# Another order of the attention units in a fused cross-attention and top-2 expert kernel, and another order of its prologue

## The chip, the cores and the metric

The kernel runs on one core of a Trainium2 chip. The metric is the device time of one execution in microseconds. Five engines work side by side, each on its own queue of instructions: TensorE (PE) for matrix products, VectorE (DVE), ScalarE (ACT), GpSimd (POOL), and SyncE (SP), which here only issues DMAs. They are kept in order by semaphores.

## What is computed

128 sequences of 64 tokens with 128 channels, float32. A causal cross-attention with 16 heads of 64, then a layer norm and a top-2 mixture of 8 experts.

```python
x = x + xattn(_layernorm(x), ctx, ctx)      # qh = q @ Wq, kh = k @ Wk, vh = v @ Wv; softmax(qh kh^T / 8, causal) vh @ Wo + bo
z = _layernorm(x'); z2 = _layernorm(z) * ln_g + ln_b   # x' = x after attention; the expert layer norms again
w = top2(softmax(z2 @ rW + rb)), normalised to 1
x = x' + z + sum_e w_e * (gelu(z2 @ W1[e] + b1[e]) @ W2[e] + b2[e])
```

## The kernel before

Two sequences make a pair of 128 tokens; there are 64 pairs, in 16 groups of four (`GP`, `NG`). Products of queries, keys and values are made of float32r parts ("high" and "low", three matmuls for one product, `split_product`, L903 to L909).

The attention work of a pair is cut into **units**, each of which fills one of five PSUM banks used in turn (`RING`). A unit's bank comes free when the unit five places earlier in `ORDER` has been evicted. The units of pair i of a group are: P (transposes of z and context, in pairs 0 and 2 only), V0 and V1 (values of the pair), K0 to K3 (in pairs 0 and 2 the queries, in pairs 1 and 3 the keys of the next two pairs), T0 and T1 (transposes of the softmax of the pair before), O0 and O1 (output of `attend` for the pair before), and the routing units RZ, RX, RL of the group before. `pair_units` (L49 to L52) writes the order; TensorE, ScalarE and VectorE each walk through it with their own code in `group`. ScalarE evicts the V, K, T and O units, makes the exponentials (`exp_half`) and seeds the score banks with the mask (`seed`). VectorE makes the maxima, differences and the normalising of the softmax. Groups 0, 1 and 15 are written out, groups 2 to 14 run in a loop on each engine.

TensorE's order for a pair n is: P, V0, `scores(n)`, `project(n-2)`, K0, T0, K1, T1, (RZ or RX), K2, K3, V1, `attend(n-1)`, (RL). `scores` (L1034) and `attend` (L1005) are 32 matmuls of 64x64 each, float32, which the profile shows as 64 records; `project` (L1018) is the product with Wo.

GpSimd normalises the inputs of the next group (`prep`), makes the rows for the experts, and sends them to DRAM with eight indirect scatters for each group, one after each unit named in `send_at` (L619). In the loop: one when the slots are known, then on O31, P0, V00, T00, O00, V10 and T11.

The prologue loads x, Wq, Wk, the context and Wv, splits the weights (ScalarE high parts L731 and L736, VectorE low parts), transposes P2 (L933, L936), transposes the small vectors b1, ln_g, ln_b (L1107), and computes eight key units before group 0. After the attention, 71 tiles of 256 rows go through the experts; that stage is not touched.

## Time and profile before

| | |
|---|---|
| three timed runs | median 1069.29 us (1067.63 to 1070.48) |
| the profiled execution | 1062.37 us, span 1060.6 us |
| busy, share of span: TensorE, VectorE, ScalarE, GpSimd | 85%, 69%, 58%, 46% |
| mean granted TensorE clock | 0.931 |

The profile is one execution. A row of the timeline says when a group of equal instructions started, how long it lasted from first start to last end, its engine, its line of the kernel, what it wrote and read, how many there were, and in brackets how long the engine stood before and what released it. "Issue" means that the profile shows nothing it waited for. A matmul's end is modelled and overlaps the next start. PEld is TensorE's weight load. SPq is the time in which the queue of SP issues a DMA.

### The profile page before, as it was taken

Reading aid. Unit: us, or ns where it says so; the run is one execution under the profiler, and the core shown is the slowest. Engines: PE = TensorE matmul, PEld = TensorE weight load, DVE = VectorE, ACT = ScalarE, POOL = GpSimd, SP = SyncE. Lnnn points to the kernel's source line nnn. Section 1 sums busy time; section 2 is a strip of 40 time slices with the busy share of each in tenths; the row PEclk is TensorE's granted clock in tenths of the full one; section 3 lists DMA queues with packets and bytes.
Section 4 is the critical chain, followed back from the end, with each engine's and each line's share of the span. In section 5 each row is a group of like instructions: output and inputs, shape, how many; then the busy total and the mean of one; then the engine's idle time right before and its main releaser. Section 6 shows DMA issues by size and latency. Waiting matters only on the chain.

```text
span 1060.6 us, 36484 instructions
## 1 busy us (share of the span) xinstructions
PE 900.8 (85%) x13361; PEld 787.1 (74%) x13361; DVE 735.7 (69%) x2239; ACT 615.3 (58%) x1317; POOL 484.4 (46%) x580
## 2 busy tenths in 40 slices
PE   5999899999999999999999999999677577777770
PEld 4889788888878888888888888888566466666660
DVE  3977787777777877777777787868376544445663
ACT  3677666666665765765675675765254243344463
POOL 3612536434363543536444363523345655555551
PEclk8999999999999999999999999999689788788885
DMA  9000101101010010101001010000123322224665
GB/s 276 23 22 2 38 16 32 32 8 35 5 37 30 13 32 8 35 8 37 30 10 35 5 35 22 13 13 10 41 61 94 89 74 73 77 78 137 171 185 193
DMA packets 55664, 56.63 MB, mean 53 GB/s; under 512 B 7335, under 2 KB 48593, under 8 KB 55601
## 3 DMA queue, kind: packets, MB, share of 16 engines
q1 hardware_dynamic: 46651, 37.94, 12.6%
q0 software_dynamic: 8640, 17.84, 5.0%
q8 instruction: 30, 0.49, 0.2%
q14 instruction: 33, 0.27, 0.1%
q10 hardware_dynamic: 310, 0.08, 0.0%
HBM read 32.62 MB, written 23.23 MB: 53 GB/s over the span
## 4 chain that ended last, share of the span: by engine, by line
PE 65%; DVE 12%; issue 10%; ACT 5%; another core or an unknown queue 5%; DMA 2%; DVEq 0%; SPq 0%; ACTq 0%; POOL 0%; POOLq 0%
PE bank L905 10%; PE bank L1018 9%; PE bank L909 9%; PE bank L906 8%; PE bank L1034 7%; PE bank L1005 7%; PE bank L1159 5%; PE bank L988 4%; DVE mx L1272 2%; PE bank L1136 2%; DVE pr L1274 2%; ACT pr L850 1%; PE bank L958 1%; PE bank L933 1%
## 5 line engine op out<-in xcount | busy, mean ns | idle before, releaser
L905 PE MATMUL bank<-in_h,Ah 128*128 128x256 f32 x654 | 213.3, 326 | 39.6 <-DVE Al L1562 12.7
L773 ACT ACTIVATE pr<-pr 128x512 f32<-128x512 f32 x128 | 80.9, 632 | 240.9 <-DVE pr L1274 240.9
L701 POOL DMA_INDIRECT mixed<-kf,ix_i x142 | 139.6, 983 | 110.5 <-DVE ix_i L1579 68.4
L905 PEld LDWEIGHTS bank<-in_h,Ah 128*128 128x128 f32 x654 | 130.2, 199 | 49.9 <-issue 21.6
L725 ACT ACTIVATE kf<-bank 128x512 f32<-128x512 f32 x256 | 155.1, 607 | 11.5 <-PE bank L909 11.1
L909 PE MATMUL bank<-in_h,Al 128*128 128x256 f32 x512 | 145.8, 285 | 0.0
L906 PE MATMUL bank<-in_l,Ah 128*128 128x256 f32 x512 | 145.4, 284 | 0.0
L615 POOL DMA_INDIRECT slots<-zrow,slot_ix x120 | 126.2, 1052 | 40.1 <-issue 28.9
L1272 DVE TENSOR_REDUCE mx<-bank 128x8 f32<-128x512 f32 x128 | 87.8, 686 | 77.1 <-PE bank L1034 76.9
L1018 PE MATMUL bank<-wo_s,oT 128*128 128x128 f32 x1024 | 135.7, 287 | 2.7 <-ACT oT L768 2.3
L550 POOL TENSOR_TENSOR idle_p<-half 128x1 f32<-128x1 f32 x114 | 26.1, 229 | 231.9 <-DVE slot_ix L1365 186.1
L1034 PEld LDWEIGHTS bank<-kf 64*64 64x64 f32 x4096 | 81.7, 137 | 66.2 <-issue 65.0
L1018 PEld LDWEIGHTS bank<-wo_s,oT 128*128 128x128 f32 x1024 | 123.2, 197 | 7.3 <-ACT oT L768 2.7
L1034 PE MATMUL bank<-kf 64*64 64x64 f32 x4096 | 101.6, 226 | 30.9 <-issue 29.5
L1284 DVE TENSOR_TENSOR pr<-pr,ri 128x512 f32<-128x512 f32 x128 | 121.3, 947 | 4.4
L1159 PE MATMUL bank<-kf,pr 128*128 128x128 f32 x568 | 96.6, 322 | 31.2 <-ACT pr L850 29.5
L1159 PEld LDWEIGHTS bank<-kf,pr 128*128 128x128 f32 x568 | 81.9, 222 | 42.2 <-ACT pr L850 31.6
L555 POOL TENSOR_TENSOR rs<-ve,half 128x4 f32<-128x4 f32 (+1 forms) x32 | 43.5, 1360 | 139.0 <-DVE ve L1213 99.7
L850 ACT ACTIVATE pr<-bank,kf 128x256 f32<-128x256 f32 x142 | 59.8, 476 | 68.9 <-remote 40.5
L906 PEld LDWEIGHTS bank<-in_l,Ah 128*128 128x128 f32 x512 | 98.8, 193 | 0.0
L909 PEld LDWEIGHTS bank<-in_h,Al 128*128 128x128 f32 x512 | 98.1, 192 | 0.0
L1274 DVE TENSOR_TENSOR pr<-bank,mx 128x512 f32<-128x512 f32 x128 | 88.5, 692 | 4.4
(191 smaller groups left out, 1949.6 us busy)
## 6 DMA issues: line engine op xcount, KB each, us to landing
kf<-slots SPq DMA_DIRECT2D x71, 130.0 KB
kf<-mixed SPq DMA_DIRECT2D x12, 512.0 KB, 3.7
xs<-in_x_dram SPq DMA_DIRECT2D x16, 256.0 KB
c_in<-in_ctx_dram SPq DMA_DIRECT2D x16, 256.0 KB
out_dram<-xs SPq DMA_DIRECT2D x16, 256.0 KB
mixed<-kf,ix_i POOLq DMA_INDIRECT x142
vf<-mixed SPq DMA_DIRECT2D x4, 512.0 KB
slots<-zrow,slot_ix POOLq DMA_INDIRECT x120
```

Of the source, the lines that this page charges most:

```text
L615: pool.indirect_dma_start(out=slots, out_offset=bass.IndirectOffsetOnAxis(ap=ix[:, k, t:t + 1], axis=0), in_=rows[:, t, :], in_offset=None ...
L701: pool.indirect_dma_start(out=mixed, out_offset=bass.IndirectOffsetOnAxis(ap=ix_i[buf][:, j:j + 1], axis=0), in_=y_sb[buf][:, j, :], in_of ...
L725: act.activation(kfs[par][:, 2 * u:2 * u + 2, :], ring[gr.bank(name)].rearrange("p (h t) -> p h t", h=2), ACT.Copy).then_inc(act_ev, 1)
L905: pe.matmul(ps, lh, rh, start=True, stop=False)
L906: pe.matmul(ps, lh, rl, start=False, stop=False)
L909: return pe.matmul(ps, ll, rh, start=False, stop=True)
L1018: last = pe.matmul(o_ps[:, 0:D], oT[:, j, :], wo_s[:, j, :], start=(j == 0), stop=(j == H // 2 - 1))
L1034: last = pe.matmul(s_ps[b][place, S * j:S * j + S], kfs[par][dims, j, toks], kfs[par][dims, H // 2 + j, toks], start=False, stop=True, ski ...
L1159: last = pe.matmul(into[:, j, :], hid[deep][:, c, j * P:(j + 1) * P], w_f[deep][:, c * D:(c + 1) * D], start=False, stop=(c == FC - 1), sk ...
L1272: dve.reduce_max(mx[:, par, hs], src, AX_X).then_inc(sm_st, 1)
L1274: dve.tensor_tensor(by_seq(par, t), src, mx[:, par, hs].unsqueeze(2).to_broadcast([P, 8, S]), ALU.subtract).then_inc(shifted, 1)
L1284: dve.tensor_tensor(by_seq(par, t), by_seq(par, t), ri[:, par, hs].unsqueeze(2).to_broadcast([P, 8, S]), ALU.mult).then_inc(probs, 1)
```

## The change

In the attention the two transposed halves of the softmax (T) come directly behind the scores of the next pair, `project` after them, and `attend` comes between K1 and K2. ScalarE's order follows, and five of the scatters are tied to other units. In the prologue the transpose of the small vectors moves behind the first scores; seven warming matmuls take its place; the product for rb joins `fold_b1`; the statistics of group 1 move to the end of the first pair on VectorE; the second x load and the load of b2 are issued earlier; ScalarE splits Wv after it has evicted P2; and GpSimd's split of W1 is cut by expert. The lines that begin with # inside the diff name the place.

```diff
 def pair_units(i):
-    return p + [v[0], k[0], t[0], k[1], t[1]] + routing + [k[2], k[3], v[1]] + o + (["RL"] if i == 2 else [])
+    return p + [v[0]] + t + [k[0], k[1]] + routing + o + [k[2], k[3]] + (["RL"] if i == 2 else []) + [v[1]]
...
+        vec_at, rb_at, b1_at = (bank[7][:, at:at + n] for at, n in ((0, E * FC + 2), (32, E), (64, E * FC)))
...
# SP, prologue (behind the two mask loads)
+            sp.wait_ge(st_ok, 9)
+            sp.dma_start(xs[:, GP:2 * GP, :], x_t[:, GP:2 * GP, :]).then_inc(ld_x, 16)
+            sp.dma_start(experts[0:3, :, 2 * HF + B2:], b2.rearrange("(a e) d -> a e d", a=1).to_broadcast([3, E, D])).then_inc(ld_v, 16)
             sp.dma_start(rb_b[:, :], rb.rearrange("(a d) -> a d", a=1).to_broadcast([P, E])).then_inc(ld_v, 16)
             sp.dma_start(rW_s[:, :], rW).then_inc(ld_v, 16)
             sp.dma_start(w1_raw[:, :, :], W1.rearrange("e d f -> d e f")).then_inc(ld_b, 16)
             sp.dma_start(wo_s[:, :, :], Wo.rearrange("(j p) n -> p j n", p=P)).then_inc(ld_w[3], 16)
-            sp.dma_start(experts[0:3, :, 2 * HF + B2:], b2.rearrange("(a e) d -> a e d", a=1).to_broadcast([3, E, D])).then_inc(ld_v, 16)
...
-            sp.wait_ge(st_ok, 9)
-            sp.dma_start(xs[:, GP:2 * GP, :], x_t[:, GP:2 * GP, :]).then_inc(ld_x, 16)
...
# GpSimd, split_w1: three instructions become 24
-                high, low = experts[:, :, 0:HF], experts[:, :, HF:2 * HF]
-                pool.tensor_scalar(low, high, gc, None, ALU.mult).then_inc(e1_ok, 1)
...
+                high, low = ([experts[:, e, at:at + HF] for e in range(E)] for at in (0, HF))
+                for e in range(E):
+                    pool.tensor_scalar(low[e], high[e], gc, None, ALU.mult).then_inc(e1_ok, 1)
+                for e in range(E):
+                    pool.wait_ge(e1_ok, e + 1)
+                    pool.tensor_copy(high[e].bitcast(F32R), low[e]).then_inc(e1_ok, 1)
+                for e in range(E):
+                    pool.wait_ge(e1_ok, E + e + 1)
+                    pool.tensor_tensor(low[e].bitcast(F32R), low[e], high[e], ALU.subtract).then_inc(e1_ok, 1)
...
# GpSimd, group loop (the same renaming before and behind the loop)
-                send_at(g - 2, group_of(g - 1), "O31", 1)
+                send_at(g - 2, group_of(g - 1), "V31", 1)
                 send_at(g - 2, gr, "P0", 2)
                 prep(g + 1, gr.done("P0"), between=lambda: send_at(g - 2, gr, "V00", 3),
-                     ahead=lambda: send_at(g - 2, gr, "T00", 4))
-                send_at(g - 2, gr, "O00", 5)
+                     ahead=lambda: send_at(g - 2, gr, "K00", 4))
+                send_at(g - 2, gr, "V01", 5)
                 x1_centre(g - 1)
                 send_at(g - 2, gr, "V10", 6)
-                send_at(g - 2, gr, "T11", 7)
+                send_at(g - 2, gr, "K11", 7)
...
# ScalarE, one pair; split_v moves behind input_unit(start, "P2", 0)
-                    exp_half(n, par, 0)
                     value_unit(gr, f"V{i}0", n, par)
+                    if attends:
+                        for t in range(2):
+                            t_unit(gr, f"T{i}{t}", n - 1, t)
+                    exp_half(n, par, 0)
                     exp_half(n, par, 1)
...
                         seed(n + 1, 0)
                     if keyed:
-                        key_unit(gr, f"K{i}2")
+                        key_unit(gr, f"K{i}1")
+                    if i == 2 and not first:
+                        r_unit(gr)
                     if seeds:
                         seed(n + 1, 1)
+                    if attends:
+                        for b in range(2):
+                            heads_unit(gr, f"O{i}{b}")
                     if keyed:
+                        key_unit(gr, f"K{i}2")
                         key_unit(gr, f"K{i}3")
                     value_unit(gr, f"V{i}1", n, par)
...
# TensorE, one pair
                     scores(n, i)
+                    if first and i == 0:
+                        vector_columns()
...
+                    if attends:
+                        for t in range(2):
+                            t_half(gr, f"T{i}{t}", n - 1, 1 - par, t)
                     if not (first and i < 2):
                         project(n - 2, gr.done(f"O{i - 1}1", 0) if i else kept.done("O31", 0))
...
                         key_unit(gr, f"K{i}0")
...
+                        key_unit(gr, f"K{i}1", (lambda: heads_free(gr, i)) if attends else None)
+                    elif attends:
+                        heads_free(gr, i)
                     if i == 2 and not first:
                         r_transposes(gr, r)
                     if i == 3 and not first:
                         r_ranks(gr, r)
+                    if attends:
+                        attend(gr, i, 1 - par)
                     if keyed:
                         key_unit(gr, f"K{i}2")
                         key_unit(gr, f"K{i}3")
...
                     if i == 2 and not first:
                         r_logits(gr)
+                    value_unit(gr, f"V{i}1", i)
+                    if not attends:
+                        fold_b1()
...
# TensorE, prologue
             input_unit(start, "P2", 0, 0)
-            pe.wait_ge(ld_v, 16 * 6)
+            warm(7)
             pe.wait_ge(pro_l, 4)
-            pe.transpose(bank[7][:, 0:E * FC + 2], vec_rows[:, :],
-                         ident[0:E * FC + 2, 0:E * FC + 2]).then_inc(vec_ps, 1)
...
# VectorE, first pair of the first group, behind its two shift halves
+                    if first and i == 0:
+                        dve.wait_ge(vec_ps, 1)
+                        dve.tensor_copy(vec_cols[:, :], vec_at).then_inc(vec_ok, 1)
+                        dve.wait_ge(vec_ok, 1)
+                        dve.tensor_copy(bc_wide[:, :], bc.to_broadcast([P, P])).then_inc(vec_ok, 1)
...
# VectorE, end of that pair
                     if first and i == 0:
-                        dve.wait_ge(fold_ps, 2)
+                        prep_stats(1)
+                        dve.wait_ge(fold_ps, 1)
+                        dve.tensor_tensor(rb_sum[:, :], rb_at, rb_b[:, :], ALU.add).then_inc(fold_ok, 1)
+                        dve.tensor_scalar(rW_g[:, :], rW_s[:, :], gc, None, ALU.mult).then_inc(w1_ok, 1)
```

## Rows read from the trace of the kernel before

**Rows 1.** Busy windows: start:end, length, busy us per engine, granted clock, DMA share, GB/s.

```profile
18.00:20.00 2.00, 1.36 (x6) 1.32 (x7) 0.93 (x5) 0.00 (x0) 0.00 (x0) 0.50 1.10 344
...
300.00:400.00 100.00, 93.27 (x1684) 82.61 (x1683) 76.19 (x209) 66.58 (x132) 46.16 (x58) 1.00 0.08 23
```

**Rows 2.** Timeline of TensorE, loop pair 0: start, us, line, tiles, count [idle before].

```profile
338.73 0.43 PE L933 MATMUL bank<-ident,z 128*128 128x128 f32 x2 [0.20 <-ACT kf L725]
...
340.01 0.92 PE L1034 MATMUL bank<-kf 64*64 64x64 f32 x40
...
342.76 2.05 PE L1018 MATMUL bank<-wo_s,oT 128*128 128x128 f32 x16
...
345.72 0.36 PE L905 MATMUL bank<-in_h,Ah 128*128 128x256 f32 x1
345.92 0.28 PE L906 MATMUL bank<-in_l,Ah 128*128 128x256 f32 x1
346.04 0.29 PE L909 MATMUL bank<-in_h,Al 128*128 128x256 f32 x1
...
349.18 1.16 PE L1005 MATMUL bank<-pT,vf 64*64 64x64 f32 x64
```

**Rows 3.** Timeline of TensorE, loop pairs 1 and 3.

```profile
305.60 0.92 PE L1034 MATMUL bank<-kf 64*64 64x64 f32 x46
...
307.34 2.05 PE L1018 MATMUL bank<-wo_s,oT 128*128 128x128 f32 x16
...
328.81 1.16 PE L1034 MATMUL bank<-kf 64*64 64x64 f32 x64
...
335.05 0.38 PE L905 MATMUL bank<-in_h,Ah 128*128 128x256 f32 x1 [0.61 <-ACT kf L725]
```

**Rows 4.** Timeline of GpSimd beside them: the indirect scatters.

```profile
305.61 0.98 POOL L615 DMA_INDIRECT slots<-zrow,slot_ix  x1 [0.48 <-issue]
...
339.42 0.98 POOL L615 DMA_INDIRECT slots<-zrow,slot_ix  x1 [0.48 <-PE bank L936]
...
340.80 0.99 POOL L615 DMA_INDIRECT slots<-zrow,slot_ix  x1 [0.16 <-issue]
...
346.80 1.43 POOL L615 DMA_INDIRECT slots<-zrow,slot_ix  x1 [0.32 <-issue]
```

**Rows 5.** Timeline of all engines, first scatter of the kernel.

```profile
105.79 1.67 POOL L615 DMA_INDIRECT slots<-zrow,slot_ix  x1 [0.65 <-issue]
...
106.40 1.39 PE L1005 MATMUL bank<-pT,vf 64*64 64x64 f32 x64
```

**Rows 6.** Timeline of all engines, prologue.

```profile
9.40 0.38 PE L936 MATMUL bank<-ident,c_in 128*128 128x128 f32 x2
...
9.71 3.78 SPq L399 DMA_DIRECT2D experts<-in_L_ffn_b_dram  x1
...
10.95 0.58 ACT L718 ACTIVATE in_h<-bank 128x512 fp32r<-128x512 f32 x1
...
11.56 0.69 DVE L1260 TENSOR_TENSOR in_l<-bank,in_h 128x512 fp32r<-128x512 f32 x1 [1.40 <-ACT in_h L718]
...
18.64 0.29 PE L1107 MATMUL bank<-ident,vec_rows 18*128 18x18 f32 x1 [8.86 <-DMA experts<-in_L_ffn_b_dram]
...
26.40 0.29 PE L1118 MATMUL bank<-rW_s,bc_wide 128*128 128x8 f32 x2
...
28.24 1.16 PE L1034 MATMUL bank<-kf 64*64 64x64 f32 x64
```

**Rows 7.** Timeline of VectorE, last step of the softmax of loop pair 1.

```profile
314.47 0.98 DVE L1284 TENSOR_TENSOR pr<-pr,ri 128x512 f32<-128x512 f32 x1
```

**Rows 8.** Timeline of all engines, last group.

```profile
747.74 0.79 PE L909 MATMUL bank<-Vh,in_l 128*128 128x512 f32 x1 [3.29 <-ACT pT L754]
...
749.68 0.69 DVE L1284 TENSOR_TENSOR pr<-pr,ri 128x512 f32<-128x512 f32 x1
...
755.21 1.06 PE L988 MATMUL bank<-ident,pr 128*128 128x128 f32 x4
```

More of the change, by code:

```diff
@@ L652, in _ @@
             send(0, upto=1)
-            send_at(0, group_of(1), "O31", 1)
+            send_at(0, group_of(1), "V31", 1)
             send_at(0, group_of(2), "P0", 2)
             prep(3, group_of(2).done("P0"), between=lambda: send_at(0, group_of(2), "V00", 3),
-                 ahead=lambda: send_at(0, group_of(2), "T00", 4))
-            send_at(0, group_of(2), "O00", 5)
+                 ahead=lambda: send_at(0, group_of(2), "K00", 4))
+            send_at(0, group_of(2), "V01", 5)
             x1_centre(1)
             send_at(0, group_of(2), "V10", 6)
-            send_at(0, group_of(2), "T11", 7)
+            send_at(0, group_of(2), "K11", 7)
             z2_rows(1)
@@ L677, in _ @@
             send(NG - 3, upto=1)
-            send_at(NG - 3, group_of(NG - 2), "O31", 1)
-            for q, name in enumerate(("P0", "V00", "T00", "O00")):
+            send_at(NG - 3, group_of(NG - 2), "V31", 1)
+            for q, name in enumerate(("P0", "V00", "K00", "V01")):
                 send_at(NG - 3, end, name, q + 2)
@@ L819, in _ @@
             input_unit(start, "P2", 0)
+            split_v()
             for k in range(4):
@@ L1051, in key_unit, with vector_columns @@
                     last = split_product(ring[gr.bank(name)][:, SUB * a:SUB * (a + 1)], Ah[:, 2 * u + a, :],
-                                         Al[:, 2 * u + a, :], in_h[par][:, src, :], in_l[par][:, src, :])
+                                         Al[:, 2 * u + a, :], in_h[par][:, src, :], in_l[par][:, src, :],
+                                         ahead if a else None)
                 last.then_inc(unit, 1)
+            def vector_columns():
+                pe.wait_ge(ld_v, 16 * 6)
+                pe.transpose(vec_at, vec_rows[:, :], ident[0:E * FC + 2, 0:E * FC + 2]).then_inc(vec_ps, 1)
             def fold_b1():
+                pe.wait_ge(vec_ok, 2)
+                pe.matmul(rb_at, bc_wide[:, :], rW_s[:, :], start=True, stop=True)
                 pe.wait_ge(ld_b, 16)
                 for u in range(E * FC):
-                    last = pe.matmul(bank[7][:, u:u + 1], w1_raw[:, u // FC, (u % FC) * P:(u % FC + 1) * P], bc,
+                    last = pe.matmul(b1_at[:, u:u + 1], w1_raw[:, u // FC, (u % FC) * P:(u % FC + 1) * P], bc,
                                      start=True, stop=True)
@@ L1074, in group @@
                     scores(n, i)
+                    if first and i == 0:
+                        vector_columns()
                     keyed = not (last and i >= 2)
+                    attends = not (first and i == 0)
+                    if attends:
+                        for t in range(2):
+                            t_half(gr, f"T{i}{t}", n - 1, 1 - par, t)
                     if not (first and i < 2):
@@ L1114, in _ @@
                 key_unit(start, f"K3{k}")
-            pe.wait_ge(vec_ok, 2)
-            pe.wait_ge(ld_w[3], 16)
-            pe.matmul(bank[7][:, 0:E], bc_wide[:, :], rW_s[:, :], start=True, stop=True).then_inc(fold_ps, 1)
             group(0, first=True)
@@ L1459, in group @@
                     n, par = GP * g + i, i % 2
-                    if i == 0 and not last:
+                    if i == 0 and not first and not last:
                         prep_stats(g + 1)
-                        if not first:
-                            mask_tables(g + 1)
+                        mask_tables(g + 1)
                     if i == 2 and not first and not second:
```

53 lines of the change are left out of this document (10 added, 43 removed).

## The prediction

> **What bounds the kernel now.** I read the busy windows first. In a stretch of the attention loop TensorE is busy 93 of 100 us at the full granted clock, VectorE 76, ScalarE 67 and GpSimd 46 [rows 1]. So only two things can change the time of the loop: what TensorE must do, and the seven per cent in which it stands still. The same view shows the second place to look: at 18 to 20 us the granted clock is 0.50 and TensorE has hardly worked.
>
> Then I read TensorE's rows for one pair [rows 2]. The 64 records of `scores` start at 340.01 and `project` follows at 342.76: 2.75 us. Undisturbed, the same 64 records take about 1.1 us (the 328.81 row lasts 1.16 with the tail of its last matmul) [rows 3]. In the next pair they take 1.74 us [rows 3]. The lost time, 1.65 and 0.65 us, has no releaser; it is "issue". I compared these places with GpSimd's rows [rows 4]. One scatter runs at 305.61, with the 1.74 us scores. Two run at 339.42 and 340.80, around the 2.75 us scores, and none is near 328.81. My reading: **while GpSimd makes an indirect scatter, TensorE gets its instructions slowly.** A store of some 35 to 45 small matmuls is used up and the rest waits until about 0.3 us after the scatter. Long matmuls hide this, a burst of 64 short ones does not. `scores` and `attend` are such bursts. The only `attend` that a scatter meets (105.79) took 1.39 instead of 1.16 us [rows 5].
>
> In the third pair the scores meet two scatters as in the first (its rows are left out; I count the same 1.65), in the fourth none. So a turn of the loop loses 0.65 + 2 x 1.65 = 4.0 us this way. In the fourth pair there is a real wait, too: K32 stands 0.61 us for ScalarE's eviction of K30 [rows 3].
>
> In the prologue the chain is short [rows 6]. TensorE has transposed P2 at 9.8 and then stands 8.86 us for the transpose of `vec_rows`, which waits for the small load of b2 (issued at 9.71, taking 3.78 us of SP). All eight key units stand behind it, and the first ones run at half clock. Scores of pair 0 start at 28.24.
>
> **The change, part by part.**
>
> *Prologue.* `vector_columns` goes behind the first scores. The first key unit then needs in_h, in_l and the weights' low parts. In_h was late, behind Vh on ScalarE (10.95); now it comes first: 9.8 + 0.58 for in_h, + 0.69 for in_l gives 11.1 [rows 6]. The seven warm matmuls add little (estimate 1.5 us from 9.8, so 11.3) and keep the clock up. Eight key units and that transpose took 26.40 - 18.64 = 7.8 us, the first half of them at clock 0.50. At the full clock a unit is six steps of 0.12 [rows 2], so eight are 5.9. P0 and V00 with the wait for kf and seeds took 1.84 (26.40 to 28.24). New start of the scores: 11.3 + 5.9 + 1.8 = 19.0, that is **-9.2**. Beside it the seeds need the mask tables, now about 14.5 (VectorE does Vl first), if the masks have landed; no row shows when. SP's order: the x load and b2 go ahead of rb, rW, W1, Wo and the expert weights, which are issued up to 4 us later (3.78 + 0.5). W1 is wanted by `fold_b1` only behind scores, four key units and V01, at about 24. Bound: between -6 (something lands late) and -10. The transposed column and the rb product only move: +0.3 in all. `prep_stats(1)` moves behind the first softmax, so GpSimd's prep(1) and its split of W1 end later against TensorE; P2 wants z about 10 us after. The split in 24 pieces lets VectorE in between; VectorE is not the bound. I take **-9.0**.
>
> *Type changes on TensorE.* The first key matmul after a transpose steps 0.20 instead of 0.12 us [rows 2]. Both transposes now follow the scores and precede `project`, so two such changes go per pair. One change comes back where `attend` is followed by K2. V1 is followed by V0 or P instead of `attend`. Over the four pairs I count -0.3 us a turn, between 0 and -0.6.
>
> *The wait in the fourth pair.* K32 takes the bank of K30, and now `attend` lies between them: 1.1 us of cover. The wait of **0.61** goes. Next late would be route_a, whose logits come 0.8 earlier because RL now stands before V21.
>
> *Scores against scatters.* The sends are renamed so that they fire at about the same moments (V31 ends the group as O31 did). Scatter 1 comes 0.7 us after the pair's start and the second one 1.4 later [rows 2, 4]. The loss in pairs 0 and 2 therefore stays. In pair 1 V10 no longer follows `attend`, so the scores start 0.1 earlier against the scatter: -0.1.
>
> *Attend against scatters.* This is new. The fifth scatter stands at 346.80, 8.07 us after the pair's start, and takes 1.43 [rows 4]. Today key units lie there, and `attend` comes at 349.18 [rows 2]. In the new order `attend` starts at 1.28 (P0, V00) + 2.75 (scores) + 2.96 (project, K00 and T00, from 342.76 to 345.72) + 0.35 (T01, as T00) + 0.8 (K01, as K00) = 8.15 [rows 2]. They meet almost exactly. The price has no row in this position. Below it is bounded by 0 (nothing is gained, since an undisturbed `attend` has no stall to lose; the store lasts: `attend` is 1.1 long and the store covers the first 0.6 to 0.8), above by 1.0 (the scatter lasts to 9.5, +0.3, +the rest). The nearest rows give 0.23 [rows 5] and 0.65 [rows 3]. I take **+0.5**.
>
> A turn: -0.61 - 0.3 - 0.1 + 0.5 = -0.5; thirteen turns are **-6.6**, between +0.3 and -13. Groups 0 and 1 run outside the loop and before the scatters: -1.2 (one wait, seven pairs of type changes).
>
> *A wait that moves.* T(n-1) is now asked right after the scores of n, and project(n-2) is queued behind it. It waits for VectorE's softmax of n-1. VectorE ends the softmax of pair 1 at 315.45, 8.1 us after its scores' end at 307.34, the longest of a turn [rows 3, 7]. A pair without lost time is about 9.5 us from scores' end to scores' end (342.76 to 349.18, then 1.1 for attend, 0.9 for V0, 1.1 for scores) [rows 2]. So at least 1.4 us of cover is left; pair 2's scores lose 1.65 more. I cost it at nothing. VectorE's addition of `project` comes 2.7 us after the scores' end and `project` now ends 2.6 after it: level.
>
> *The end.* In the last group no keys fill TensorE. V31 waits 3.29 us for pT [rows 8], because ScalarE takes the exponentials of the last pair before the transposes. The new order takes the transposes first. Next late is then RX, which waits for the routing, and after that the transposes of pair 63: its softmax ends at 750.4, while they start at 755.21 today behind project(62) [rows 8]. So no more than 4.8 us can go here. The scatters of group 14 still meet the last `attend`. I take **-3.5**, between 0 and -4.8.
>
> The expert stage is untouched and moves as a whole. **Sum:** -9.0 - 1.2 - 6.6 - 3.5 = -20.3. The profiled execution took 1062.4 us (span 1060.6), which gives 1042.1. It lies 6.9 us below the median of the timed runs, 1069.3; against that the forecast is 1069.3 - 20.3 = **1049**.
>
> A page speaks of the same "issue" time. The Trainium skill, "Runtime: NRT & Kernel Launch", section "Instruction fetch mechanics", says that each engine fetches its code in 16 KiB blocks and that an issue floor of about 20 cycles an instruction hides the fetching. By that rule bursts would run at the pace of the issuing side, and two bursts close together (`attend`, then `scores`) would run it dry, scatter or none. The undisturbed row [rows 3] has an `attend` just before it, too, and doesn't agree. The rival that follows from the rule is the first below.
>
> **The rivals.**
> 1. *The store is not full when the scores begin,* because `attend` emptied it 1 to 2 us before. Then putting K2, K3 and V1 between the bursts as well, 15 long matmuls, heals both. For: each disturbed burst of scores follows an `attend`. Against: the attend of rows 5 follows no burst and still lost time. It would give back 4.0 and the 0.5 a turn: 13 x 4.5 = 59, so 990. Chance 0.08.
> 2. *Attend pays in full* (1.0 a turn: +6.5) and the end gives nothing (+3.5): 1059. Chance 0.15.
> 3. *The prologue's gain is not there,* since masks, seeds or W1 arrive no earlier (they come behind the attention weights in the queue), and rival 2 as well: 1067 to 1069. Chance 0.08.
> 4. *Slower: the transposes in front.* If VectorE's softmax is more than 1.4 us later than today against TensorE (GpSimd's tensor work holding it up, a later `project` holding the addition), T and with it project, keys and all wait in each pair. It decides from 1.4 us on; each further us costs about 60 us over the 63 pairs. With 0.5 us over it: 1049 + 30 = 1079. For: project and K0, 2.6 us, no longer cover the wait. Against: TensorE is busy 93% and VectorE 76% [rows 1]. Chance 0.09.
>
> My forecast has 0.60, with a range of its own of 1042 to 1056.
>
> **How the numbers follow.** The low end takes attend at 0 (-6.5), the end at -4.8 and the prologue at -10: 1040. The high end holds rival 2 and a prologue of -6: 1061. Left out are rival 1, rival 4 and most of rival 3. About 0.3% (3 us) is what a measurement of this kernel can tell from no change. Faster: forecast, rivals 1 and 2 and a little of 3: 0.84. Same 0.07, slower 0.09.
>
> **What would show it.** Prologue: first key matmul near 11.3, first scores near 19, granted clock 1.00 between 10 and 20 us. Loop: a turn shorter by 0.5 us; no wait at K32; scores of pairs 0, 1 and 2 as long as today; the attend of pair 0 about 1.6 long with an "issue" gap. End: no 3.29 us wait for pT. I am wrong if the scores lose no time any more (rival 1), if T waits for VectorE (rival 4), or if scatters have moved onto other bursts.

## The result and the profile after

The changed kernel is slower. Its median is 1078.25 us of 9 runs (1073.58 to 1081.31); the kernel before, run beside it, has 1069.29 (1065.42 to 1070.92). The ratio is 1.011, with a 95% interval of 1.0086 to 1.0134. I had forecast 1049 and faster. Where the executions of a kernel fall into two sets, as those of project_first and fifth_scatter_later do below, medians and ratios are of the faster set (eight of twelve, 1057.8 to 1070.6 us, and five of twelve, 1049.4 to 1061.9; the others reach 1088.5 and 1076.7, one stands at 2735.6).

The profiled execution of the changed kernel took 1076.2 us, its span is 1074.4. That is 13.8 us over the span of the kernel before (1060.6). Four moments split these 13.8 us: the first scores, the first scores of the loop, the last scores, and the first matmul of the expert stage. Timeline of TensorE, changed kernel (start, length, engine, line, operation, count):

```profile
18.85 1.16 PE L1038 MATMUL bank<-kf 64*64 64x64 f32 x64
...
99.10 0.90 PE L1038 MATMUL bank<-kf 64*64 64x64 f32 x37
...
751.05 1.16 PE L1038 MATMUL bank<-kf 64*64 64x64 f32 x64
...
780.22 1.06 PE L1143 MATMUL bank<-ident,kf 128*128 128x128 f32 x4
```

The same moments of the kernel before (the first is the 28.24 of [rows 6]):

```profile
113.19 1.56 PE L1034 MATMUL bank<-kf 64*64 64x64 f32 x48
...
738.78 1.16 PE L1034 MATMUL bank<-kf 64*64 64x64 f32 x64
...
768.28 1.06 PE L1136 MATMUL bank<-ident,kf 128*128 128x128 f32 x4
```

| stretch | before | after | difference | forecast |
|---|---|---|---|---|
| to the first scores | 28.24 | 18.85 | -9.4 | -9.0 |
| groups 0 and 1 | 84.95 | 80.25 | -4.7 | -1.2 |
| loop and last group | 625.59 | 651.95 | +26.4 | -6.6 |
| last scores to expert stage | 29.50 | 29.17 | -0.3 | -3.5 |
| expert stage | 292.3 | 294.2 | +1.9 | 0 |

So the prologue did what it should, and everything is lost in the loop. A turn of the loop (four pairs) took 45.6 us and takes 47.8 now; these are medians of the 13 turns of each profiled execution.

Pair 0 shows most of it. TensorE of the changed kernel, scores of pair 0 to the attend behind them; this stretch answers to [rows 2]:

```profile
523.72 0.81 PE L1038 MATMUL bank<-kf 64*64 64x64 f32 x40
524.84 0.31 PE L1038 MATMUL bank<-kf 64*64 64x64 f32 x2 [0.31 <-issue]
525.59 0.30 PE L1038 MATMUL bank<-kf 64*64 64x64 f32 x2 [0.44 <-issue]
526.34 0.61 PE L1038 MATMUL bank<-kf 64*64 64x64 f32 x20 [0.45 <-issue]
526.88 1.97 PE L990 MATMUL bank<-ident,pr 128*128 128x128 f32 x8
528.64 2.74 PE L1022 MATMUL bank<-wo_s,oT 128*128 128x128 f32 x16
531.14 0.36 PE L907 MATMUL bank<-in_h,Ah 128*128 128x256 f32 x1
...
532.73 1.22 PE L1007 MATMUL bank<-pT,vf 64*64 64x64 f32 x54
534.30 0.42 PE L1007 MATMUL bank<-pT,vf 64*64 64x64 f32 x10 [0.35 <-issue]
```

Beside it GpSimd, the indirect scatters:

```profile
523.49 0.99 POOL L615 DMA_INDIRECT slots<-zrow,slot_ix  x1 [0.48 <-PE bank L938]
...
524.87 0.99 POOL L615 DMA_INDIRECT slots<-zrow,slot_ix  x1 [0.16 <-issue]
...
532.93 1.35 POOL L615 DMA_INDIRECT slots<-zrow,slot_ix  x1 [0.48 <-issue]
```

Two things are to be seen. The scores take 3.16 us to the next operation, 2.75 before: the first scatter starts 0.23 us ahead of them and not 0.59, so the second one, too, ends later against the burst, and the burst ends about 1.0 us after the second scatter in both kernels (525.86 to 526.88; 341.79 to 342.76). Pairs 1 and 2 show the same: their scatters start 0.20 and 0.34 us later against the scores than before, and the bursts are 0.17 and 0.38 us longer. And behind the burst the transposes and the projection last 1.97 and 2.74 us. In the next group of rows the reason stands: the granted clock is 0.50 there (526.90). Busy windows of the changed kernel (start:end, length, busy us per engine, granted clock, DMA share, GB/s):

```profile
200.00:700.00 500.00, 464.87 (x7891) 419.27 (x7893) 367.52 (x1034) 332.18 (x628) 217.74 (x273) 0.97 0.07 21
...
146.40:149.80 3.40, 3.40 (x40) 3.33 (x32) 2.92 (x6) 2.05 (x4) 3.20 (x5) 1.00 0.32 103
...
526.90:530.30 3.40, 3.40 (x18) 3.40 (x17) 3.09 (x5) 1.92 (x4) 3.20 (x5) 0.50 0.28 77
```

and of the kernel before, the loop and the stretch behind the same scores (340.01):

```profile
200.00:700.00 500.00, 466.13 (x8308) 413.50 (x8307) 387.54 (x1089) 331.71 (x659) 227.48 (x285) 1.00 0.07 23
...
342.70:346.10 3.40, 3.40 (x37) 3.34 (x30) 3.18 (x6) 1.60 (x3) 3.20 (x5) 1.00 0.27 87
```

The changed kernel falls to the lower of the two clock levels (1.2 for 2.4 GHz) in the last eleven of the 13 turns of the loop and once more in the last group, each time behind pair 0's scores; in the kernel before no fall starts in the loop. From the first transpose to the first key matmul it is 4.26 us (526.88 to 531.14); in pair 1 of the group before, at the full clock, the same steps take 2.63 (491.85 to 494.48). A fall costs 1.6 us. The second turn of the changed kernel says the same: its scores of pair 0 (143.35) are held up as long, 3.01 us, the clock stays at 1.00 behind them (146.40 above), and the turn takes 46.1 us; the next one has a fall and takes 47.7.

A turn with a fall then adds up, pair by pair (scores to scores, before and after): 11.2 and 13.95, 10.6 and 10.7, 12.6 and 13.0, 11.2 and 10.1. By cause: +1.6 for the clock; +0.95 for longer scores in pairs 0, 1 and 2 (first to last start 3.04, 1.80, 3.16 us for 2.64, 1.63, 2.78; 0.94 undisturbed); +0.83 for the attend of pair 0 (1.77 for 0.94), which the scatter at 532.93 meets; -1.1 in pair 3, where the waits at K32 and P0 are gone. That is +2.3 of the measured +2.2.

### The profile page after: what moved, and what is told of

Same layout as the page of the kernel before. It is cut to its first block, busy times and chain, and to the rows that moved or that the text cites. A ratio compares the mean times of both kernels' runs of the same rounds, so it can differ in the third digit from the quotient of the medians.

```text
span 1074.4 us, 36492 instructions
## 1 busy us (share of the span) xinstructions
PE 914.0 (85%) x13368; PEld 811.1 (75%) x13368; DVE 729.0 (68%) x2239; ACT 636.8 (59%) x1317; POOL 488.1 (45%) x601
## 4 chain that ended last, share of the span: by engine, by line
PE 75%; issue 8%; another core or an unknown queue 6%; DVE 5%; ACT 3%; DMA 1%; POOL 1%; DVEq 0%; POOLq 0%; ACTq 0%; SPq 0%
PE bank L1022 11%; PE bank L907 11%; PE bank L911 9%; PE bank L908 9%; PE bank L1038 9%; PE bank L990 7%; PE bank L1007 7%; PE bank L1166 5%; PE bank L1143 2%; ACT pr L852 1%; PE bank L960 1%; PE bank L1161 1%; PE bank L935 1%; PE bank L938 1%
## 5 line engine op out<-in xcount | busy, mean ns | idle before, releaser
L907 PE MATMUL bank<-in_h,Ah 128*128 128x256 f32 x654 | 207.7, 318 | 24.5 <-DVE Al L1569 10.8
L728 ACT ACTIVATE kf<-bank 128x512 f32<-128x512 f32 x256 | 148.0, 605 | 26.0 <-PE bank L911 20.5
L756 ACT ACTIVATE pT<-bank 128x512 f32<-128x512 f32 x128 | 70.9, 595 | 152.3 <-PE bank L990 152.3
L615 POOL DMA_INDIRECT slots<-zrow,slot_ix x120 | 126.0, 1050 | 42.3 <-issue 30.8
L1038 PEld LDWEIGHTS bank<-kf 64*64 64x64 f32 x4096 | 84.2, 135 | 76.0 <-issue 75.8
L1038 PE MATMUL bank<-kf 64*64 64x64 f32 x4096 | 105.7, 226 | 40.7 <-issue 40.7
L1022 PEld LDWEIGHTS bank<-wo_s,oT 128*128 128x128 f32 x1024 | 131.9, 208 | 10.5 <-ACT oT L770 10.5
L1291 DVE TENSOR_TENSOR pr<-pr,ri 128x512 f32<-128x512 f32 x128 | 110.4, 863 | 4.4
```

Of the source, the lines that this page charges most:

```text
L615: pool.indirect_dma_start(out=slots, out_offset=bass.IndirectOffsetOnAxis(ap=ix[:, k, t:t + 1], axis=0), in_=rows[:, t, :], in_offset=None ...
L728: act.activation(kfs[par][:, 2 * u:2 * u + 2, :], ring[gr.bank(name)].rearrange("p (h t) -> p h t", h=2), ACT.Copy).then_inc(act_ev, 1)
L907: pe.matmul(ps, lh, rh, start=True, stop=False)
L1022: last = pe.matmul(o_ps[:, 0:D], oT[:, j, :], wo_s[:, j, :], start=(j == 0), stop=(j == H // 2 - 1))
L1038: last = pe.matmul(s_ps[b][place, S * j:S * j + S], kfs[par][dims, j, toks], kfs[par][dims, H // 2 + j, toks], start=False, stop=True, ski ...
L1291: dve.tensor_tensor(by_seq(par, t), by_seq(par, t), ri[:, par, hs].unsqueeze(2).to_broadcast([P, 8, S]), ALU.mult).then_inc(probs, 1)
```

## The experiments

All ratios are to the kernel before, run on the same chip. A turn is read between the scores of pair 0 in consecutive groups of the profiled execution; the table has the median of the 13 turns of the loop, and in how many of them the clock fell. The kernel before has 45.6 and 0, the changed kernel 47.8 and 11.

| kernel | median us | ratio, 95% interval | turn | turns with a fall |
|---|---|---|---|---|
| prologue_alone | 1057.7 | 0.992 (0.9892 to 0.9949) | 45.7 | 1 |
| changed_again | 1077.0 | 1.0097 (1.0066 to 1.0129) | 47.7 | 13 |
| project_first | 1063.2 | 0.9974 (0.9944 to 1.0004) | 46.1 | 2 |
| fifth_scatter_later | 1057.6 | 0.9919 (0.9883 to 0.9956) | 47.7 | 11 |
| both_small | 1041.6 | 0.9749 (0.9725 to 0.9774) | 44.4 | 0 |
| two_moved | 1020.9 | 0.962 (0.9594 to 0.9645) | 44.4 | 8 |
| tail_held | 1059.6 | 0.9992 (0.9967 to 1.0018) | 47.6 | 11 |
| after_retimed | 1009.6 | 0.9492 (0.9459 to 0.9526) | 42.3 | 0 |
| after_clean | 1015.8 | 0.9581 (0.9555 to 0.9607) | 43.6 | 1 |
| after_spaced | 1001.9 | 0.9376 (0.9352 to 0.9401) | 42.1 | 1 |
| first_order_clean | 1040.6 | 0.9816 (0.9793 to 0.9839) | 44.9 | 3 |
| first_order_spaced | 1053.8 | 0.9874 (0.9853 to 0.9895) | 45.8 | 1 |
| exps_first | 1091.7 | 1.0242 (1.0216 to 1.0267) | 48.5 | 11 |
| first_order_exps_later | 1036.2 | 0.9712 (0.9687 to 0.9737) | 44.5 | 0 |

**The parts and the clock.**

```diff
 project_first: in every pair
-t_half(T0), t_half(T1); project(n - 2)
+project(n - 2); t_half(T0), t_half(T1)
 fifth_scatter_later (both_small: this and the one above)
-ahead=lambda: send_at(g - 2, gr, "K00", 4)
+ahead=lambda: send_at(g - 2, gr, "K02", 4)
```

prologue_alone is the kernel before with the prologue's part of the diff.

> The kernel before with the prologue of the change and nothing of its new order of attention. In the trace of the changed kernel the first scores start at 18.85 us, before at 28.24. Theory A (the prologue is a plain gain, the loss is all in the order of attention): the 9.4 us stay, ratio to the kernel before about 0.991 (1060 us), loop turns of 45.6 us as before. Rival (the gain is given back in the first two groups, where other work comes due earlier, or the shorter prologue brings clock falls): ratio 1.000, time 1069 us.

Measured: 0.992, turns as before. About 8 of the 9.4 us are kept to the end. The loss comes with the rest of the diff, the new order and the scatters tied to other units.

> The changed kernel as it is, beside the others on this chip, with its own profile. If the clock falls of the loop belong to the kernel, this execution shows them again, once per turn of 47.8 us, and the ratio is 1.011. If they were chance, they are fewer here, turns without a fall take 46.1 us, and the ratio is nearer 1.000.

Measured: 1.0097, turns of 47.7 us, mean clock 0.97 between 200 and 700 us as in the first profile. The falls belong to this kernel; here they start with the first turn of the loop and not with the third.

> The changed kernel with one swap: in every pair the output projection (16 matmuls of 128x128) again stands ahead of the transposes of the probabilities. In the changed kernel the granted clock falls to half for 3.4 us once in each loop turn, at the transposes behind the scores of pair 0; in the kernel before it doesn't. Theory A (the fall comes from what follows the held-up scores: transposes and short work where a long run of full matmuls stood): no falls in the loop, about 1.7 us less per turn, 12 turns, some -20 us: ratio to before 0.992 (1058 us). Rival B (the fall comes from the held-up scores themselves, 3.04 us long now against 2.64 before, whatever follows): falls stay, ratio stays 1.011 (1078 us).

Measured: 0.9974, against an expected 0.992, turns of 46.1 us, and in the profiled execution no clock fall from the fourth turn of the loop on. The second and the third turn still have one each, behind pair 0's scores, and take 47.7 us:

```profile
200.00:700.00 500.00, 469.54 (x8228) 420.17 (x8227) 381.84 (x1071) 329.87 (x654) 216.31 (x278) 1.00 0.07 21
149.30:152.70 3.40, 3.40 (x19) 3.40 (x18) 2.48 (x5) 0.00 (x0) 2.95 (x4) 0.50 0.23 76
...
517.68 1.25 PE L1038 MATMUL bank<-kf 64*64 64x64 f32 x42
...
520.13 0.60 PE L1038 MATMUL bank<-kf 64*64 64x64 f32 x20 [0.46 <-issue]
520.66 2.05 PE L1022 MATMUL bank<-wo_s,oT 128*128 128x128 f32 x16
522.55 1.04 PE L990 MATMUL bank<-ident,pr 128*128 128x128 f32 x8
```

The scores are still held up (2.84 us here, 2.87 in most turns, from first to last start), yet the clock stays. So a held-up burst alone doesn't bring the fall. What the swap takes away is the clock: from the second turn on, those without a fall are 46.1 us long in both orders. But theory A, that the work behind the burst decides, isn't shown either. The swapped order fell twice, behind bursts of 2.86 and 2.90 us, and the changed order did not fall in its second turn, behind 3.01.

> The changed kernel with one word changed: the fifth indirect scatter of a group waits for the third key unit of pair 0 and not for the first, so that it doesn't run during pair 0's output product (attend), which takes 1.75 us under it and 0.94 us elsewhere. Theory A (a scatter holds up only the bursts of 64x64 matmuls it overlaps, and the time goes straight into the turn): attend of pair 0 back at 0.94, about -0.8 us per turn, 13 turns: -11 us, ratio to before 1.001 (1067 us). Rival (the next scatters move back in time with it and hold up the scores of pair 1 longer, or the clock fall moves): less than -3 us, ratio 1.008 to 1.011.

Measured: 0.9919, some 20 us less than the changed kernel, where theory A had 11. Its attend of pair 0 is at 0.94, and the scores of pair 1, too (0.94 for 1.80), which I had not counted: 1.7 us a turn and 13 turns give 22 us. The profile must be read with care, since it is of an execution of 1076.1 us, 18 us above the median of those behind the ratio. In it a turn takes 47.7 us, and eleven turns have a second fall, behind pair 2's scores (at 503.2, for instance). The two turns without any fall take 44.5 and 44.4 us.

> The changed kernel with both small edits of the first set together: projection ahead of the transposes, and the fifth scatter of a group at K02 and not at K00. The first alone had no clock fall in the loop and turns of 46.0 us, the second alone freed pair 0's attend (0.94 for 1.75) and the scores of pair 1 (0.94 for 1.80), but had two clock falls in a turn of 47.8 us. Theory A (the two costs add: 0.8 + 0.85 us of held-up bursts, and the falls): turns of 44.4 us, 1065 - 13 x 1.6 = 1044 us, ratio 0.978. Rival B (what one fall gives back another takes, since they depend on where a held-up burst meets the clock): falls again, turns of 46 us or more, ratio 0.995 or above.

Measured: 0.9749, turns of 44.4 us, clock 1.00 in the loop. Theory A met its number: the costs of the held-up bursts add up. 46.1 - 1.7 is 44.4.

**The scatters.** What was changed is only which unit of TensorE each scatter waits for (q1 to q7) and, with it, where GpSimd's normalisation (`prep`) stands among them.

```diff
 two_moved (q1, q2, q3)
-V31, P0, V00
+T01, T01, T01
 after_retimed (q1 to q7)
-V31, P0, V00, K00, V01, V10, K11
+T01, T01, K02, K02, T11, T11, K12
 after_spaced, in the loop (send_after_scores waits for sc_ps)
-send_at(V31, 1); send_at(P0, 2); prep(g + 1, between V00 3, ahead K00 4); send_at(V01, 5)
-x1_centre(g - 1); send_at(V10, 6); send_at(K11, 7)
+send_after_scores(pair 0, 1); send_after_scores(pair 0, 2); prep(g + 1, ahead K01 3)
+send_after_scores(pair 1, 4); send_after_scores(pair 1, 5); send_at(K11, 6); send_at(K11, 7)
+x1_centre(g - 1)
 its end, as in tail_held
-send(NG - 2)
+send(NG - 2, upto=1); pool.wait_ge(unit, tail.done("O01")); send_rows(zrow, slot_ix, 1, 2 * GP)
```

> The changed kernel, with only the second and third scatter of a group moved, from the end of the turn (V31, P0) to behind the transposes of pair 0 (T01), so that pair 0's scores stand free; the scatters on pair 0's attend and on the scores of pairs 1 and 2 stay. Theory A (pair 0's held-up scores cost 2.1 us and are also what makes the clock fall behind them): pair 0's scores 0.94, no clock fall, -3.8 us per turn, 13 turns: -49 us, ratio to before 0.965. Rival B (the clock falls come from any held-up burst at an unlucky moment): they move behind pair 1 or 2, only -2.1 us per turn: -27 us, ratio 0.986. Rival C (the moved scatters lengthen pair 0's attend by as much as the scores win): no change.

Measured: 0.962. Three scatters were moved and not two, as the diff shows, and those behind them came later, too. So pair 0's scores are at 0.94, but its attend (1.0) and pair 1's scores (0.94) stand free as well; only pair 2's scores are held up as before (3.0 to 3.6). Turns without a fall take 42.8 us. The falls did not go with pair 0's hold-up: eight turns have one, the first seven and one later, now behind pair 2's scores (297.30 to 300.4, fall at 300.4). So B is right on the falls, A on the size, by a different sum.

> The changed kernel with the same eight scatters per group, but q1 to q7 of them waiting for other units (T01, T01, K02, K02, T11, T11, K12), so that they run beside the projection, keys and values and not beside scores or attend. Theory A (scatters hold up the bursts of small matmuls and nothing else; the clock fall follows from a held-up burst): all bursts at 0.94 us, which takes 2.1 + 0.83 + 0.86 + 2.2 = 6.0 us out of a turn, and no clock fall, 1.7 us: turns of about 40.1 us instead of 47.8, 13 turns -100 us, about 978 us, ratio 0.915. Rival B (the scatters slow the full matmuls they then lie on as much): time stays at 1078 us. Rival C (VectorE or ScalarE, busy 35 us of a turn, sets the pace as soon as TensorE is relieved): turns of 43 to 45 us, 1015 to 1045 us, with new waits of the transposes for the softmax.

Measured: 0.9492, turns of 42.3, no fall in the loop. Theory B is refuted, and this is the main finding: with most of the same scatters beside full matmuls 5.5 us of a turn are gone, 1.6 of it the clock. Of theory A's 7.7 the bursts still held up explain 2.1: pair 0's attend (1.77 us), pair 1's scores (2.06) and its attend (1.09), each for 0.94.

> The changed kernel with all scatters placed beside full matmuls: q1, q2 at T01, q3, q4 at K01, then the normalisation of the next group, q5, q6 at T11, q7 at K11; and the last group's seven held as in tail_held. The retimed kernel measured before this one still had pair 0's attend at 1.75 and pair 1's scores at 2.0 us, turns of 42.2 us and 1009.6 us. Theory A: another 0.8 + 1.1 + 0.15 us per turn and 9 us at the end: turns of 40.2 us, 1009.6 - 13 x 2.0 - 9 = 975 us, ratio 0.915. Rival C (another engine sets the pace from about 42 us a turn): 1009.6 - 9 = 1000 us, with TensorE waiting for VectorE's or ScalarE's results.

Measured: 0.9581, worse than the kernel it was to improve, turns of 43.6. The longest turn, 44.9 us with the only fall, shows one reason. The normalisation behind q4 held GpSimd to 506.1, q5 to q7 came late and met pair 1's attend:

```profile
504.84 1.28 POOL L583 TENSOR_TENSOR xs<-xs,bo_b 128x512 f32 x1
...
506.44 1.05 POOL L615 DMA_INDIRECT slots<-zrow,slot_ix  x1 [0.17 <-issue]
...
507.88 1.00 POOL L615 DMA_INDIRECT slots<-zrow,slot_ix  x1 [0.16 <-issue]
```

That attend starts at 507.91 and takes 3.18 us for 0.94. In the other turns of the loop it takes between 1.0 and 3.0, and TensorE waits for ScalarE besides, for instance 0.69 us at 414.97 for the eviction of oT.

> The changed kernel with the scatters sent as: q1, q2 behind pair 0's scores, q3 behind K01, q4, q5 behind pair 1's scores, q6, q7 behind K11, the normalisation of the next group between q2 and q4, the last seven held. In after_clean the POOL engine came late with q5 to q7, since the normalisation stood behind q4, and they fell on pair 1's attend (3.18 us for 0.94); in after_retimed two bursts of a turn of 42.2 us still stood at 1.75 and 2.0 us. Theory A (nothing else is behind the turn): all bursts at 0.94, turns of 40.2 us, 1009.6 - 26 - 9 = 975 us, ratio 0.917. Rival C (from about 42 us a turn VectorE or ScalarE sets the pace): 1000 us, ratio 0.940, and TensorE waits for their results between the bursts.

Measured: 0.9376, the fastest kernel of the study. From the second turn of the loop on every burst takes 0.94 us and the clock is 1.00 (in the first one attend takes 3.58, with a fall), but a turn is 42.1 and not 40.2. The 1.2% over after_retimed go with the held end. TensorE's waits between 300 and 600 us (waiter, releaser: sum, times, longest):

```profile
PE bank L917 <- ACT kf L738: 3.5, 7, 0.5
PE bank L917 <- DVE in_l L1277: 2.3, 7, 0.3
PE bank L921 <- ACT kf L738: 1.5, 7, 0.2
```

They are 7.3 us in seven turns, 1.0 a turn. But such a row counts from the modelled end of the matmul before, and in an undisturbed row the next start lies ahead of that end. From start to start, beside the same turn of after_retimed, the three places cost more. In the turn from 566.71, V20 loses 0.5 us (586.08), the first key matmul behind the projection 0.6 (590.82) and the one behind attend 0.6 (594.53); 0.3 more comes at the second key unit there, and 1.9 is all that is missing. So theory C is right: with the bursts free, ScalarE's evictions and VectorE's low parts come too late in pair 2.

**The end.**

> The changed kernel, with seven of the last group's eight back-to-back scatters held until the last output product (attend) is done. In the changed kernel that product takes its operands at 765.32 us and signals at 775.5, 1.5 us after the last of the seven scatters ends at 774.0; alone it takes 0.94. Theory A (the scatters hold it up): it signals after about 1 us, the output projection behind it starts at about 768 and not at 776.65, so about -9 us in front of the expert stage: ratio to before 1.003 (1069 us) if the clock falls of the loop stay. Rival (the time goes back into the wait: what follows needs the scatters' data or POOL's work behind them): less than -2 us.

Measured: 0.9992 against 1.0097 and 1.011 for the changed kernel. Timeline of the changed kernel first, of tail_held below:

```profile
765.32 0.97 PE L1007 MATMUL bank<-pT,vf 64*64 64x64 f32 x49 [0.74 <-ACT pT L756]
765.35 1.06 POOL L615 DMA_INDIRECT slots<-zrow,slot_ix  x1 [3.25 <-issue]
...
773.04 0.96 POOL L615 DMA_INDIRECT slots<-zrow,slot_ix  x1 [0.30 <-issue]
...
775.51 1.09 ACT L770 ACTIVATE oT<-bank 128x512 f32<-128x512 f32 x2 [10.25 <-remote]
...
776.65 3.78 PE L1022 MATMUL bank<-wo_s,oT 128*128 128x128 f32 x16 [8.11 <-ACT oT L770]
```

```profile
763.09 1.16 PE L1009 MATMUL bank<-pT,vf 64*64 64x64 f32 x64 [0.74 <-ACT pT L758]
764.30 1.08 ACT L772 ACTIVATE oT<-bank 128x512 f32<-128x512 f32 x2 [1.26 <-PE bank L1009]
765.44 2.05 PE L1024 MATMUL bank<-wo_s,oT 128*128 128x128 f32 x16 [1.19 <-ACT oT L772]
766.14 0.97 POOL L615 DMA_INDIRECT slots<-zrow,slot_ix  x1 [6.28 <-issue]
```

Seven scatters in a row keep the last attend from ending for 10.2 us; with them behind it, ScalarE goes on 1.2 us after its start. The expert stage begins at 767.3 for 780.2. Of these 12.9 us, 9.0 lie between attend and its eviction, 1.7 in the projection, which ran at the lower clock in the changed kernel (3.78 for 2.05), and 2.2 ahead of attend: the loop was 0.9 shorter, and the fall in the last group lasted half as long. In the changed kernel the 64 recorded starts end at 768.3, and ScalarE is released only at 775.5; what holds the rest back has no row.

**Why the old order wins nothing.** first_order_clean and first_order_spaced keep the old order of TensorE and ScalarE, with the new prologue, and only move the scatters.

> The order of attention of the kernel before (projection behind the scores, attend last) with the new prologue, the scatters of a group moved off the bursts (q1 to q3 at K00, q4 to q7 at K10) and the last seven held. It tells what the new order of attention is worth once no scatter meets a burst. Theory A (the order is nearly worth nothing by itself: 0.6 + 0.3 us of waits per turn, which the traces show of TensorE for ScalarE): within 5 to 15 us above after_clean. Rival (the new order hides the softmax better, since TensorE would otherwise wait as soon as turns get shorter): over 20 us above it. Rival the other way (the first order is as good or better): at or below it. In numbers: turns of 45.6 - 1.7 - 0.7 - 1.8 = 41.4 us, about 1057.7 - 13 x 4.2 - 5 = 998 us, ratio 0.936.

Measured: 0.9816, turns of 44.9, with pair 1's attend at 3.4 to 3.5 us and pair 0's at 1.9. It is 25 us above after_clean, which is the rival's case.

> The order of attention of the kernel before with the new prologue and the scatters sent right behind the scores: q1 to q4 behind pair 0's, q5 to q7 behind pair 1's, the last seven held. In first_order_clean four of them still fell on pair 1's attend (3.5 us). All bursts at 0.94 should give turns of 45.6 - 4.2 = 41.4 us. Theory A (the new order itself is worth 0.9 us of TensorE's waits for ScalarE per turn, and the old one has nothing worse): 1057.7 - 55 - 5 = 998 us, 12 to 20 us above after_spaced. Rival (the new order hides the softmax of a shorter turn, which the old one can't): over 30 us above after_spaced. Rival the other way: at or below after_spaced.

Measured: 0.9874, turns of 45.8, with every burst at 0.94 in most turns. It is 52 us above after_spaced, so the rival is right and theory A wrong: 4.2 us of hold-ups are gone and the turn is no shorter than in prologue_alone (45.7). TensorE's waits between 300 and 600 us in it, and below in the kernel before:

```profile
PE bank L924 <- ACT pT L768: 10.7, 10, 1.9
PE bank L920 <- ACT kf L740: 8.5, 14, 0.7
PE bank L920 <- DVE in_l L1280: 6.7, 7, 1.2
```

```profile
ACT pr L773 <- DVE pr L1274: 99.4, 53, 4.1
...
PE bank L1034 <- issue: 14.7, 33, 0.7
PE bank L905 <- ACT kf L725: 3.7, 6, 0.6
```

The 25.9 us of waits, 4 a turn, take the place of the hold-ups. ScalarE's 99.4 us say where they come from: in the old order the exponentials, which wait for VectorE, stand ahead of the evictions. In the changed kernel that wait is 12.7 us. Two more kernels move the exponentials alone:

```diff
 exps_first = after_spaced, ScalarE's queue in a pair
-V0; T0, T1; exp, exp; K0
+exp; V0; exp; T0, T1; K0
 first_order_exps_later = first_order_spaced
-exp; V0; exp; K0; T0
+V0; K0; T0; exp, exp
```

> after_spaced (ratio 0.938, turns of 42.1 us, no held-up burst) with one thing put back on ScalarE: the two exponentials of a pair stand ahead of the evictions of V0, T0 and T1 again, as in the kernel before. TensorE's order stays the new one. Theory A (the exponentials wait for VectorE, and what is queued behind them on ScalarE comes late for TensorE; this is what the new order removed): most of the 4 us a turn goes again, turns of 45 to 46 us, ratio 0.975 to 0.990, with TensorE waiting for pT or for free banks. Rival (TensorE's order does it, with the attend between the key units and the transposes right behind the scores): turns of 42 to 43 us, ratio 0.938 to 0.950.

Measured: 1.0242, some 90 us above after_spaced. The turns run from 47.0 to 52.1 us, 48.9 in the mean. The two without a fall take 47.0, so the order of ScalarE alone costs 4.9 us a turn, near what I had expected; the rest comes with clock falls, 13 in eleven turns, most of them at the wait for pT in pair 0. ScalarE and TensorE of exps_first at this place, in its longest turn:

```profile
546.70 0.63 ACT L785 ACTIVATE pr<-pr 128x512 f32<-128x512 f32 x1 [4.81 <-DVE pr L1291]
...
548.02 0.63 ACT L785 ACTIVATE pr<-pr 128x512 f32<-128x512 f32 x1 [0.21 <-DVE pr L1291]
548.55 1.06 ACT L766 ACTIVATE pT<-bank 128x512 f32<-128x512 f32 x2
...
549.84 0.52 PE L921 MATMUL bank<-in_h,Al 128*128 128x256 f32 x1 [2.80 <-ACT pT L766]
```

The exponential waits 4.81 us for VectorE, pT is evicted behind it, and TensorE stands 2.80 us inside K1, in front of attend. In the turn from 249.44, which has no fall, TensorE stands 1.81 us there.

> first_order_spaced (ratio 0.987, turns of 46.2 us, no held-up burst) with the two exponentials of a pair moved on ScalarE behind the evictions of V0, K0 and T0. TensorE's order stays that of the kernel before. Theory A (as for exps_first): TensorE's waits for pT and kf shrink, turns of 43 to 44 us, ratio 0.955 to 0.965. Rival (TensorE's order does it): turns of 46 us, ratio 0.985 to 0.990. Third case (later exponentials make the softmax late, and the transposes wait for VectorE): above 0.990.

Measured: 0.9712, turns of 44.5. The direction is theory A's, the size is not: 1.2 us of the 3.6 a turn between first_order_spaced and after_spaced come back. Of the other 2.4, 0.6 is a hold-up, since the first scatter now meets pair 3's attend (1.5 us for 0.94). The rest goes with TensorE's order and what is left of the differences in ScalarE's; no run separates them.

## Why the prediction was wrong, point by point

- **Prologue, -9.0: right.** First key matmul at 11.19 (forecast 11.3), first scores at 18.85 (19.0), granted clock 1.00 from 0 to 20 us. prologue_alone keeps it to the end. Groups 0 and 1 gave 4.7 and not 1.2; prologue_alone takes 85.1 us for them, the kernel before 84.95, so the 4.7 come with the new order.
- **The waits of the fourth pair, -0.6: right,** and P0's wait went, too.
- **Attend of pair 0, +0.5: right in place, short in size.** It met the fifth scatter as worked out; the price is 0.83, between my 0.5 and the 1.0 of rival 2. The prediction says that the attend at 105.79 is the only one that a scatter meets. That is wrong: the last attend of the kernel before meets four of them, and its rows show a price far above the bound of 1.0 (at the lower clock, which it has from 759.9 on, a free burst takes 1.7 us):

```profile
757.60 1.22 PE L1005 MATMUL bank<-pT,vf 64*64 64x64 f32 x42 [0.69 <-ACT pT L754]
...
763.57 1.09 ACT L768 ACTIVATE oT<-bank 128x512 f32<-128x512 f32 x2 [6.02 <-PE bank L1005]
```

- **"The sends fire at about the same moments, the loss therefore stays": wrong.** The scatters start 0.36, 0.20 and 0.34 us later against the scores of pairs 0, 1 and 2, and the three bursts are together 0.95 us a turn longer, nearly one for one.
- **No term for the clock: the largest error.** The view of windows showed 1.00 in the loop, and I took that for a property of the loop. With the new order the clock falls behind the held-up scores in eleven turns of the loop and in the last group, at 1.6 us each about 19 us. This turned the sign. With only two falls in the loop (project_first, 0.9974) the kernel is level with the one before and not faster by what I forecast.
- **The end, -3.5: wrong.** The wait of 3.29 for pT [rows 8] went. But the last attend came nearer to the start of the burst of scatters: in the kernel before it needs 5.97 us (757.60 to the eviction at 763.57), with four scatters under way or to come, now 10.2, with seven. I wrote that the scatters "still meet the last attend" and didn't cost how many.
- **My reading of the hold-ups: right, its use incomplete.** Scatters moved off the bursts free them (after_retimed, two_moved, after_spaced). I didn't ask what the hold-ups covered. In the old order they lay over waits for ScalarE, which first_order_spaced shows; in the new order such waits are small, and the hold-ups enter the turn almost in full (46.1 to 42.3 in after_retimed, for 3.9 us of hold-ups fewer), down to about 42 us a turn, where the waits of pair 2 take their place (after_spaced). So the change removed about 4 us a turn of hidden waits and gained nothing from it, since it left TensorE alone with the hold-ups.
- **Rival 1 (the store is emptied by the attend in front): refuted.** In the new order K2, K3, V1 and V0 stand between attend and every burst of scores, and pair 0's scores are held up for longer. In first_order_spaced attend (528.50) and scores (530.49) follow each other within 2 us and both take 0.94, so two bursts near each other do not run dry by themselves. The Trainium skill, "Runtime: NRT & Kernel Launch", section "Instruction fetch mechanics", says only that the issue floor hides the fetching; that two bursts would run dry was my own inference and not the page's.
- **Rival 4 had the right time (1079) and the wrong mechanism.** No transposes wait for VectorE in the loop; the time is the clock and the hold-ups.

## What to carry to other kernels

If an engine's rows show stretches of "issue" beside a scatter of GpSimd, treat the scatter as a user of that engine, and place it beside its long instructions before reordering anything. A reorder that removes waits pays only as far as nothing else holds the same engine; ask of each existing stall which waits it hides. Compare turns with and without a clock fall before putting a price on an order, and read more than one turn. On ScalarE, an instruction that waits for VectorE belongs behind the evictions that TensorE needs.

## What the runs showed of the hardware

- Under two scatters a burst of 64 records of 64x64 matmuls mostly takes 2.5 to 3.2 us from first to last start instead of 0.94. It goes on in small groups 0.7 to 0.8 us apart and ends 0.7 to 1.0 us after the second scatter. Full matmuls beside a scatter show no such gap: in after_spaced two scatters (526.65 and 528.03) lie on the projection and K0 of pair 0, and the projection takes 1.95 us as elsewhere, the key matmuls step by 0.12.
- The hold-up seems to go with the making of the scatter and not with its data; one place shows it. In the changed kernel's last group the held-up scores go on at 743.48, while GpSimd waits until 744.58 for the data of the scatter that its row ends at 743.09:

```profile
742.10 0.99 POOL L615 DMA_INDIRECT slots<-zrow,slot_ix  x1 [0.16 <-issue]
...
744.58 1.03 POOL L564 TENSOR_TENSOR zrow<-xp,rs 128x512 f32<-128x512 f32 x1 [1.49 <-DMA slots<-zrow,slot_ix]
```

  The Trainium skill, "Perfetto Trace Analysis", section "DMA Instruction — SWDGE (GPSIMD)", says that such a row ends when the descriptors are made and not when the data has moved; the trace agrees. What keeps small matmuls from starting meanwhile has no row in any trace.
- The granted clock can fall inside a loop in which TensorE is busy 93% of the time, once or twice per turn, mostly for about 3.4 us and at a price of 1.6. The falls of the changed kernel, of tail_held and two_moved start behind a held-up burst; the single one in the loop of first_order_spaced (390 us) behind a wait of 1.85 us for pT. Neither the length of the hold-up nor the order decides: the changed kernel has 3.01 us without a fall and 3.04 with one in the next turn, project_first 2.90 with one and 2.87 without. tail_held has the same loop as the changed kernel, and yet its falls lie behind pair 2's scores in eight turns, behind pair 0's in three, and two turns have none. What decides is open.
